# Cross-attention with top-k rows on one core: input 6 is scored by VectorE, the key-bias term is computed by VectorE, and the second query projection stands behind the second weighted sum

## The reference, cut to what matters

```python
scores = einsum('bnd,d->bn', base_hidden, score_w[0]) + score_b[0]     # 8 inputs x 224 rows x 512
_, topk_idx = top_k(scores, 10)
sparse_hidden = take_along_axis(base_hidden, topk_idx[:, :, None], axis=1)
q = sparse_hidden @ Wq.T + bq        # 10 rows, 16 heads of 32
k = scaffold_hidden @ Wk.T + bk      # 750 context rows
v = scaffold_hidden @ Wv.T + bv
logits = einsum('bhqd,bhkd->bhqk', q, k) * scale
attn = softmax(logits)
o = einsum('bhqk,bhkd->bhqd', attn, v)
attn_out = o @ out_w.T + out_b
return base_hidden.at[arange(B)[:, None], topk_idx].set(attn_out)
```

## Time and profile before

| what | value |
|---|---|
| median of 3 runs | 140.95 us (140.5 to 141.01) |
| profiled execution, its own time | 140.47 us |
| span of that execution | 138.7 us |
| TensorE busy | 132.0 us (95%) |
| VectorE busy | 91.7 us (66%) |
| ScalarE busy | 27.0 us (19%) |
| GpSimd busy | 10.9 us (8%) |
| granted TensorE clock, mean | 1.000 |
| DMA | 37.52 MB, 270 GB/s mean |

### The profile page before, as it was taken

The page is one execution under the profiler, slowest core; times in us unless marked ns, Lnnn a source line. Parts: engine busy times, 40 slices in busy tenths (PEclk is TensorE's granted clock), DMA queues, the critical chain, the costliest instruction groups (busy, mean ns, idle before and its releaser), DMA issues.

```text
span 138.7 us, 3144 instructions
## 1 busy us (share of the span) xinstructions
PE 132.0 (95%) x1314; PEld 125.6 (91%) x1314; DVE 91.7 (66%) x252; ACT 27.0 (19%) x59; POOL 10.9 (8%) x36
## 2 busy tenths in 40 slices
PE   6889999999998999999999999999999999999990
PEld 3168999999997899999999999999999999999970
DVE  4596697898993676487872565177228799875160
ACT  5132400070511250012140041004101400131120
POOL 7710000260030000000000000000000000000002
PEclk9999999999999999999999999999999999999999
DMA  3999999999614999799999897998795093000001
GB/s 68 405 427 416 409 405 405 414 443 428 268 40 129 425 426 419 291 343 316 395 379 294 319 438 224 318 409 308 240 285 217 5 322 131 0 0 5 0 5 50
DMA packets 7293, 37.52 MB, mean 270 GB/s; under 512 B 1040, under 2 KB 1040, under 8 KB 5104
## 3 DMA queue, kind: packets, MB, share of 16 engines
q1 hardware_dynamic: 6864, 37.00, 70.6%
q0 software_dynamic: 128, 0.33, 0.8%
q10 hardware_dynamic: 288, 0.01, 0.1%
HBM read 33.50 MB, written 3.83 MB: 269 GB/s over the span
## 4 chain that ended last, share of the span: by engine, by line
PE 63%; DVE 14%; DMA 13%; SPq 4%; issue 4%; POOLq 1%; POOL 0%; DVEq 0%
PE mix_ps L899 29%; PE logits_ps L862 24%; DMA x_sb<-x_lines_dram 11%; PE logits_ps L846 5%; DVE product L442 3%; DMA picked<-x_dram,row_idx 2%; DVE col_max L569 2%; SPq L220 2%; PE logits_ps L818 2%; DVE probs L603 1%; PE mix_ps L818 1%; SPq L209 1%; DVE q_diag L530 1%; POOLq L62 1%; PE logits_ps L784 1%
## 5 line engine op out<-in xcount | busy, mean ns | idle before, releaser
L899 PE MATMUL mix_ps<-probs,ctx_r 125*128 125x160 f32 x336 | 47.2, 300 | 0.0
L899 PEld LDWEIGHTS mix_ps<-probs,ctx_r 125*128 125x128 f32 x336 | 46.0, 190 | 0.3 <-issue 0.2
L862 PE MATMUL logits_ps<-qk,ctx_c 128*125 128x160 f32 x240 | 33.4, 299 | 0.0
L862 PEld LDWEIGHTS logits_ps<-qk,ctx_c 128*125 128x125 f32 x240 | 32.9, 188 | 0.0
L569 DVE TENSOR_REDUCE col_max<-logits_ps 125x160 f32<-125x480 f32 x16 | 10.1, 653 | 16.6 <-PE logits_ps L862 13.7
L846 PE MATMUL logits_ps<-qk,ctx_c 128*125 128x160 f32 x144 | 20.1, 300 | 0.0
L846 PEld LDWEIGHTS logits_ps<-qk,ctx_c 128*125 128x125 f32 x144 | 19.6, 188 | 0.1
L388 ACT ACTIVATE mix<-mix_ps 128x320 f32<-128x320 f32 x16 | 7.0, 440 | 62.7 <-PE mix_ps L899 57.7
L610 DVE TENSOR_REDUCE prob_sum<-probs 125x160 f32<-125x960 f32 x8 | 14.6, 1829 | 4.5 <-ACT probs L378 4.4
L378 ACT ACTIVATE probs<-probs 125x480 f32<-125x480 f32 x16 | 9.3, 602 | 25.3 <-DVE probs L603 25.3
L442 DVE CUSTOM_DVE_ANT_0 product<-x_sb,score_w_sb 112x513 f32<-112x513 f32 x14 | 10.0, 761 | 2.4 <-DMA x_sb<-x_lines_dram 2.4
(11 more groups left out here) (137 smaller groups left out, 100.0 us busy)
## 6 DMA issues: line engine op xcount, KB each, us to landing
ctx_r<-ctx_rows_dram SPq DMA_DIRECT2D x7, 1536.0 KB, 10.2
ctx_c<-ctx_cols_dram SPq DMA_DIRECT2D x6, 1500.0 KB, 8.9
x_sb<-x_lines_dram SPq DMA_DIRECT2D x8, 520.0 KB, 13.0
out_dram<-x_sb SPq DMA_DIRECT2D x8, 448.0 KB, 9.7
ctx_r<-ctx_rows_dram SPq DMA_DIRECT2D x3, 512.0 KB, 15.5
ctx_c<-ctx_cols_dram SPq DMA_DIRECT2D x2, 750.0 KB, 14.4
ctx_c<-ctx_cols_dram SPq DMA_DIRECT2D x4, 375.0 KB, 15.1
wq_sb<-wq_dram SPq DMA_DIRECT2D x1, 1024.0 KB, 8.0
```

Source lines behind the costliest of these rows:

```text
L862: last = nc.tensor.matmul(logits_ps[n][0:S_P, t // BANK_T, (t % BANK_T) * HQ:(t % BANK_T + 1) * HQ], ctx_c[n][:, f, t, :], qk[:, b, f, :], ...
L899: last = nc.tensor.matmul(mix_ps[half][:, f * HQ:(f + 1) * HQ], ctx_r[n][0:S_P, t, c:c + P], probs[n][:, t, :], start=(t == 0), stop=(t == ...
```

## The change

Three things are edited. GpSimd's products and ScalarE's sums of input 6 go, and VectorE does `score(6)` between the subtraction of input 0 and `score(7)`. The key-bias term is computed by VectorE alone, from the queries spread by head: product with the bias (`key_terms`), a transposing sum, three copies to bring the four quadrants together, a small sum; TensorE's `dot_key_bias` goes, and `key_heads` with it. For group 0 this stands ahead of `score(2)`; for group 1 behind `copy_pairs`. The second projection stands behind all of `weigh(1)`, and the transposes move from before tile 18 to before tile 21. Group 1's queries are biased and spread by one instruction for each of the four column blocks e (128x240), out of PSUM into `q_pairs`, in the order head, input, query; the fold reads them permuted, and waits in its step 0 for one e after the other.

```diff
@@ gpsimd
-            pool.memset(key_heads[:, :, :], 0.0).then_inc(heads_cleared, 1)
-            pool.wait_ge(x_in[POOLED], 16)
-            for j in range(2):
-                if j:
-                    pool.wait_ge(multiplied, j)
-                pool.tensor_tensor(out=pool_product[j], in0=x_sb[0:X_P, POOLED, j, 0:D + 1], in1=score_w_sb[:, :],
-                                   op=ALU.mult).then_inc(multiplied, 1)
@@ scalar
-            sum_products()
@@ vector
+            def spread_pairs():
+                b0, b1 = GROUPS[1]
+                nb = b1 - b0
+                for e in range(DT):
+                    dve.wait_ge(q_ps, 3 + e // 2)
+                    nc.vector.scalar_tensor_tensor(
+                        out=q_pairs[:, e, :, :, :].rearrange("p h b q -> p h (b q)"),
+                        in0=query_ps[1][e // 2][:, (e % 2) * nb * TOPK:(e % 2 + 1) * nb * TOPK]
+                        .unsqueeze(1).broadcast_to([P, HPT, nb * TOPK]),
+                        scalar=bias_sb[:, 0, e:e + 1],
+                        in1=head_mask[:, :].unsqueeze(2).broadcast_to([P, HPT, nb * TOPK]), op0=ALU.add, op1=ALU.mult)\
+                        .then_inc(pair_q_done, 1)
+            def first_key_terms():
+                dve.wait_ge(q_done, 2)
+                nc.vector.tensor_tensor(
+                    key_terms[:, 0:FIRST, :, :, :].rearrange("p b e h q -> p e b (h q)"),
+                    q_diag[0][:, :, :, :, :].rearrange("p e b h q -> p e b (h q)"),
+                    bias_sb[:, 1, :].unsqueeze(2).unsqueeze(3).broadcast_to([P, DT, FIRST, HC]), ALU.mult).then_inc(key_terms_done, DT)
+            def pair_key_terms():
+                dve.wait_ge(pair_q_done, DT)
+                for e in range(DT):
+                    nc.vector.tensor_scalar(key_terms[:, FIRST:B, e, :, :].rearrange("p b h q -> p h b q"), q_pairs[:, e, :, :, :],
+                                            bias_sb[:, 1, e:e + 1], None, ALU.mult).then_inc(key_terms_done, 1)
+            def sum_key_terms(g):
+                b0, b1 = GROUPS[g]
+                bs = slice(b0, b1)
+                at = 4 * g
+                dve.wait_ge(key_terms_done, DT * (g + 1))
+                nc.vector.tensor_reduce(
+                    quad_sum[:, 0, bs, :].rearrange("p b k -> p (b k)"),
+                    key_terms[:, bs, :, :, :].rearrange("p b e h q -> p (b e h q)").rearrange("p (k c) -> p k c", c=QUAD),
+                    AX.X, ALU.add, apply_transpose=True).then_inc(key_step, 1)
+                dve.wait_ge(key_step, at + 1)
+                for q in range(1, QUADS):
+                    nc.vector.tensor_copy(quad_sum[0:QUAD, q, bs, :], quad_sum[q * QUAD:(q + 1) * QUAD, 0, bs, :]).then_inc(key_step, 1)
+                dve.wait_ge(key_step, at + 4)
+                nc.vector.tensor_reduce(key_dot[:, bs, :], quad_sum[0:QUAD, :, bs, :].rearrange("p q b k -> p b k q"), AX.X, ALU.add)\
+                    .then_inc(key_dot_done, 1)
@@ vector, order
-            nc.vector.tensor_tensor(key_heads[:, :, 0:HPT], bias_sb[:, 1, :].unsqueeze(2).broadcast_to([P, DT, HPT]),
-                                    head_mask[:, :].unsqueeze(1).broadcast_to([P, DT, HPT]), ALU.mult).then_inc(key_heads_done, 1)
-            spread_queries(0)
+            spread_queries()
+            first_key_terms()
+            sum_key_terms(0)
             score(2)
-            spread_key_dot(0)
...
             subtract_max(0, 0)
+            score(6)
             score(7)
...
-            spread_queries(1)
+            spread_pairs()
             copy_pairs()
-            spread_key_dot(1)
+            pair_key_terms()
+            sum_key_terms(1)
@@ tensor
-                pe.wait_ge(scored, 2 * (b1 - 1))
-                pe.wait_ge(summed, 2)
+                pe.wait_ge(scored, 2 * b1)
...
-                pe.wait_ge(q_done, 4)
...
                     for e in range(DT):
+                        if step == 0:
+                            pe.wait_ge(pair_q_done, e + 1)
...
-                                                    q_diag[1][rows, e, :, 2 * r:2 * r + 2, :],
+                                                    q_pairs[rows, e, 2 * r:2 * r + 2, :, :].rearrange("p h b q -> p b h q"),
...
-            dot_key_bias(0)
             logits_by_step(0, 0, [qk_done], {})
-            pe.wait_ge(key_rows_done, DT)
             logits_by_step(1, 1, [], {})
             weigh_by_part()
-            weigh(1, 1, {18: transpose_picked, 21: lambda: project_queries(1)})
+            weigh(1, 1, {21: transpose_picked})
+            project_queries(1)
             fold_pairs()
-            dot_key_bias(1)
```

More of the change, by code:

```diff
@@ L113, in build @@
         picked_T = [sb(f"picked_T{g}", [P, DT, b1 * TOPK]) for g, (b0, b1) in enumerate(GROUPS)]
-        q_diag = [sb(f"q_diag{g}", [P, DT, b1 - b0, HPT, TOPK])
-                  for g, (b0, b1) in enumerate(GROUPS)]
-        q_sb = [sb(f"q_sb{g}", [P, DT, b1 - b0, TOPK]) for g, (b0, b1) in enumerate(GROUPS)]
+        q_diag = [sb("q_diag0", [P, DT, FIRST, HPT, TOPK])]
+        q_pairs = sb("q_pairs", [P, DT, HPT, GROUPS[1][1] - GROUPS[1][0], TOPK])
+        q_sb = sb("q_sb", [P, DT, FIRST, TOPK])
         qk = sb("qk", [P, B, QK_STEPS, HQ])
-        key_heads = sb("key_heads", [P, DT, QUAD])
-        key_rows = sb("key_rows", [QUAD, B, DT, HC])
-        inv_rows = key_rows[:, :, :, :].rearrange("p b e c -> p b (e c)")
+        key_terms = sb("key_terms", [P, B, DT, HPT, TOPK])
+        inv_rows = key_terms[0:QUAD, :, :, :, :].rearrange("p b e h q -> p b (e h q)")
         key_dot = sb("key_dot", [QUAD, B, CB])
@@ L530, in spread_queries @@
                     nc.vector.tensor_tensor(
-                        q_diag[g][:, es, :, :, :].rearrange("p t b h q -> p (t b) h q"),
-                        q_sb[g][:, es, :, :].rearrange("p t b q -> p (t b) q").unsqueeze(2).broadcast_to([P, 2 * nb, HPT, TOPK]),
-                        head_mask[:, :].unsqueeze(1).unsqueeze(3).broadcast_to([P, 2 * nb, HPT, TOPK]), ALU.mult)\
+                        q_diag[0][:, es, :, :, :].rearrange("p t b h q -> p (t b) h q"),
+                        q_sb[:, es, :, :].rearrange("p t b q -> p (t b) q").unsqueeze(2).broadcast_to([P, 2 * FIRST, HPT, TOPK]),
@@ L819, in fold_pairs @@
                                                     wk_sb[rows, e, step * P:(step + 1) * P],
-                                                    q_diag[1][rows, e, :, 2 * r:2 * r + 2, :],
+                                                    q_pairs[rows, e, 2 * r:2 * r + 2, :, :].rearrange("p h b q -> p b h q"),
                                                     start=True, stop=True)
                     last.then_inc(pair_done, 1)
-            def dot_key_bias(g):
-                w = TOPK * (GROUPS[g][1] - GROUPS[g][0])
-                pe.wait_ge(key_heads_done, 1)
-                pe.wait_ge(q_biased, 2 * g + 2)
-                for e in range(DT):
-                    last = nc.tensor.matmul(key_ps[g][e * QUAD:(e + 1) * QUAD, 0:w], key_heads[:, e, :],
-                                            q_sb[g][:, e, :, :].rearrange("p b q -> p (b q)"), start=True, stop=True)
-                last.then_inc(key_dot_ps, 1)
             def logits_by_step(b, n, copied, between):
```

50 lines of the change are left out of this document (9 added, 41 removed).

## The result

| | before | after |
|---|---|---|
| median | 140.53 us (15 runs) | 139.47 us (15 runs) |
| profiled execution, its own time | 140.47 us | 139.39 us |
| span | 138.7 us | 137.6 us |

The ratio is 0.9925, 95% interval 0.9912 to 0.9939: 1.06 us faster. The forecast was 1.02 less and 139.93; with more runs the kernel before has a median of 140.53 and not 140.95, and that is 0.42 of the 0.46 between 139.93 and 139.47. The profiled execution, forecast at 139.45, took 139.39.

The account below looks back on a forecast made before the run. TensorE, full from 64.23 to 129.54, made the start of input 2's logits decisive. Gather +0.14, tiles and wait -1.14, dot products -0.24, stall +0.22 gave -1.02, so 139.93 us, range 139.4 to 140.8.

Parts of the forecast that it names:

- What bounds the kernel: TensorE is full from 64.23 to 129.54, so the start of input 2's logits, 51.09 before, decides.
- A, the gather: Up to the gather: two more VectorE products +1.22, GpSimd collision gone -1.08, so the gather lands 0.14 later.
- Rival 1: GpSimd did not hold the second product, or scorings come no cheaper: gather 1.22 late, 141.0 us; chance 0.10.
- key terms of group 0: VectorE's added work before input 5 lands: no cost, as VectorE waits until 21.68 anyway.
- The transposes: TensorE ready at 42.53, gather at 42.56: transposes start 0.14 later, the wait before them nearly gone.
- B, order and spread: From transposes to input 2's logits, 8.67 before: -1.14 tiles and wait, -0.24 dot, +0.22 stall.
- The 1.14 for tiles and wait: Between second projection and fold: three tiles and a wait, 1.14 in all, both go if VectorE is ready.
- the stall: In the fold's step 0, TensorE waits for the last spread block, e3, ready at 46.80: 0.22 lost.
- Rival 2: VectorE's 128x240 spread operation is dear, up to 0.66 instead of 0.42: 140.8 us; chance 0.10.
- Rival 3: The fold slows because its moving operand comes in runs of 10 elements: slower, up to 144.6 us; chance 0.05.
- Key terms of group 1: On VectorE behind copy_pairs: 3.7 us, from 50.6 to 54.3, leaving 1.8 of cover before find_max(2).
- Rival 4: The saving is made and lost, because a load or VectorE's chain is late next: 140.9 us; chance 0.07.

Follow-up runs that it names:

- only_scores: The kernel before with only input 6's scoring moved to VectorE, GpSimd and ScalarE not doing it: 140.72 us, ratio 1.0004.
- gpsimd_reads: The changed kernel with GpSimd's two products of input 6 put back, used by nobody: 140.55 us, ratio 1.0004 to the kernel before.
- quadrant_read: The changed kernel plus one unused 32x1 VectorE copy from PSUM partitions 96 to 127, before the last q_diag: 139.65 us, ratio 0.9942 to the kernel before.
- changed_again: The changed kernel run once more, unaltered, for comparison on the same chip: 139.59 us, ratio 0.9933 to the kernel before.
- only_order: The kernel before with only the order changed: transposes before tile 21, second projection behind the last tile of weigh(1): 140.55 us, ratio 1.0006.
- after_wait_all: The changed kernel with the fold waiting for all four spread blocks before its first matmul: 140.28 us, ratio 0.9988 to the kernel before.
- bank_per_e: The changed kernel with the second projection done block by block, each with its own PSUM bank and signal: 138.97 us, ratio 0.9894 to the kernel before.
- tile_behind: The changed kernel with the last tile of the second weighted sum put back behind the second projection: 139.34 us, ratio 0.991 to the kernel before.

## Why the prediction was right

**What bounds the kernel.** Right: only the stretch from the transposes to the logits of input 2, and the landing of the gather, moved the end. The start of the logits moved by 1.16 and the span by 1.17, and the 87.64 us behind it stayed as they were. A further witness is the head of the changed kernel's trace: input 0 landed 0.69 earlier there (first product at 5.13 instead of 5.82), the logits of input 0 began 0.79 earlier, and none of it reached the end; it was waited away, in part before the rows' landing:

```profile
29.21 2.20 PEld L867 LDWEIGHTS mix_ps<-probs,ctx_r 125*128 125x128 f32 x16 [0.16 <-DMA ctx_r<-ctx_rows_dram]
```

**A, the gather.** The mechanism was right in both terms. Two products more, one collision less: +0.14 forecast, +0.16 measured, and shown in both directions: with GpSimd's products taken out alone 0.14 (only_scores), with them put back 1.08 (gpsimd_reads). Rival 1 falls: the long product is gone with GpSimd's products and returns with them. The gather came 0.12 earlier and not 0.14 later, for two things that I did not have: the landings of that execution (0.11 and 0.05), and 0.12 from `key_rows` no longer being the last to read PSUM (quadrant_read). I had said that the key terms of group 0 cost and bring nothing because VectorE then waits for input 5 anyway; they brought these 0.12, behind that wait.

**The transposes.** I had TensorE ready at 42.53 and the gather at 42.56, so the idle time nearly gone: 0.17 was left in one execution and 0.35 in another (changed_again). The three tiles moved ahead took 0.81 (0.82 forecast), but TensorE had come to them earlier than I had reckoned, since input 0 had landed early, and was ready at 42.13. The direction was right.

**B, order and spread.** The 1.14 for tiles and wait was read from the trace before, and all of it went. The condition that I gave for it (if VectorE is ready) was the right one: with the old spread it is all given back (only_order), with the new one but a single wait it is mostly given back (after_wait_all). The term that was mis-sized is the stall: 0.22 forecast, 0.35 measured. The operation takes 0.46, and 0.38 from start to start where nothing is waited for (44.78, 45.17), so my 0.42 was between the two. The third operation started at 45.72, 0.12 after the projection's last issue, the fourth at 46.10. That puts block 3 at 46.56, within 0.02 of where the prediction had it once the 0.26 of the earlier gather are taken off (46.80 less 0.26). The time at which it was ready was right; the price that I put on it was too low. Three things correct it. By the prediction's own times the stall was 0.19 (46.80 less 46.61) and not 0.22; adding 0.42 to its 46.36 would even have given 46.78 and 0.17. The loads of block 3 are due 0.66 behind the fold's first, not 0.75: in bank_per_e, where none waits, they stand at 46.12 and 46.78. And they start 0.05 after the operation that makes the block has ended, for which I had put nothing. With these the same sum gives 0.33 (0.19, 0.09 and 0.05), close to the 0.35. TensorE's weight loads of the changed kernel for blocks 2 and 3, each from a narrow window:

```profile
46.24 0.30 PEld L815 LDWEIGHTS logits_ps<-q_pairs,wk_sb 64*128 64x128 f32 x4
46.61 0.30 PEld L815 LDWEIGHTS logits_ps<-q_pairs,wk_sb 64*128 64x128 f32 x4
```

Rival 2 falls (0.46, not 0.66).

VectorE's spread operations in the changed kernel (line, duration ns min/median/max, first and last start us):

```profile
L514 DVE SCALAR_TENSOR_TENSOR q_pairs<-logits_ps,bias_sb,head_mask x4: 458/464/469, 44.8 to 46.1; 128x240 f32<-128x240 f32 x4
```

**The fold's operand.** Rival 3 falls: steps 2 to 4 take 1.0 us, as before with runs of 20, and with bank_per_e the first too.

**Key terms of group 1.** Forecast 3.7 us of work and 1.8 of cover; VectorE's rows of the changed kernel:

```profile
50.61 1.10 DVE L541 TENSOR_SCALAR key_terms<-q_pairs,bias_sb 128x240 f32<-128x240 f32 x4
51.75 1.18 DVE L549 TRANSPOSE_TENSOR_REDUCE quad_sum<-key_terms 128x30 f32<-128x960 f32 x1
52.96 0.57 DVE L555 COPY quad_sum<-quad_sum 32x30 f32<-32x30 f32 x3
53.56 0.35 DVE L557 TENSOR_REDUCE key_dot<-quad_sum 32x30 f32<-32x120 f32 x1
...
55.94 0.66 DVE L566 TENSOR_REDUCE col_max<-logits_ps 125x160 f32<-125x480 f32 x1 [2.02 <-PE logits_ps L834]
```

3.3 of work (50.61 to 53.91) and 2.02 of idle time left: it costs nothing. Rival 4 falls too: no wait of a later stage took the saving, as the unchanged 87.64 us say.

**How much of the agreement is luck.** The mechanism was right in every term that was forecast, but the closeness of the sum is in part luck: the stall cost 0.13 more than forecast, and the 0.12 between input 5's product and `quad_max`, which I had put at nothing, came back for it. The landings of this execution then gave 0.16 that changed_again (0.97 instead of 1.16) does not have.

**What is open.** The spread by blocks in the old order was not run. So it isn't shown how much it brings alone. My estimate is 0.13: three tiles then still stand between projection and fold, the last of their records starts at 46.50 in the trace before, and in tile_behind, where VectorE's first block is long ready, the fold starts 0.23 behind such a record (45.65 to 45.88); so the fold could have started at 46.73 and not at 46.86. GpSimd was shown to hold VectorE up with an instruction that reads two inputs and not with one that only writes; one with a single input was not run. And whether transposes before tile 22 are worth their shorter path in time is not settled.

## What to carry to other kernels

Work that is put between a producer and its consumer to fill a wait is worth moving only when the wait itself gets shorter: here the order alone gave nothing, the wait by blocks alone is estimated at 0.13, and the two together gave 0.80 us from the transposes to the logits. When the consumer reads in blocks, let the producer finish whole blocks, in banks of their own, and signal each: in that stretch it gave 0.34 us more than the change, the largest further step that is shown (138.97 us). And look at what runs beside a long instance of an instruction before moving work off an engine: here VectorE could take over GpSimd's share for almost nothing (0.14 us for 1.22 of work) only because the collisions had cost nearly as much as the work.

## What the runs showed of the hardware

- GpSimd's two-input product and VectorE's two-input product take turns: VectorE's takes 1.76 us instead of 0.69 when it waits, GpSimd's 1.65 to 1.83 instead of 1.28. Seven memsets of GpSimd over the same stretch leave VectorE's products at 0.68 and 0.69. So it is not GpSimd's writing that holds VectorE up; by these runs its reading is what is left.
- A read of PSUM from partition 96 nine microseconds earlier costs the next VectorE instruction that reads PSUM from partition 0 its overlap with its predecessor, 0.12 us (2.61 against 2.48); seen in three kernels whose `key_rows` do it and in one with a single-column copy.
- VectorE's operation with a scalar and two inputs, one from PSUM and broadcast, 128x240: 0.46 us, 0.38 apart when nothing is waited for. With one input from SBUF and a scalar, 128x240: 0.34 us.
- TensorE's fold runs at the same pace with a moving operand in runs of 10 elements as in runs of 20 (1.0 us for a step of 16 records of 120 columns).
